# Last layer of a four-part transformer kernel: constant column addresses for TensorE, the weights' transfers placed sooner in SyncE's queue, their splitting placed later on ScalarE and VectorE

## What is computed

```python
# hidden_states = _layernorm(x): 2048 rows of 512
queries = (hidden_states @ W_q).reshape(2, n, 64)
routing = jnp.einsum('tnd,tdk->tnk', queries, keys)          # 2 x n x 64
scores2, idx2 = jax.lax.top_k(routing, 8)
...
scores, pk = jax.lax.top_k(all_scores, 8)                     # the best 8 of 8 x 8 sums
indices = jnp.take_along_axis(all_idx, pk, axis=-1)
de, ue = down_embed[indices], up_embed[indices]               # 8 rows of 512 per token, twice
ew = jnp.einsum('nh,nkh->nk', x, de)
ew = jax.nn.silu(ew) * jax.nn.softmax(scores, axis=-1)
experts_states = jnp.einsum('nk,nkh->nh', ew, ue)
mlp = jax.nn.silu(x @ gate_w) * (x @ up_w) @ down_w           # 512 -> 2048 -> 512
return mlp + experts_states
```

## Time and profile before

| | us |
|---|---|
| median of three runs (2124.6 to 2127.25) | 2127.24 |
| profiled execution, its own time | 2129.43 |
| its span, first to last instruction | 2127.6 |
| TensorE busy in the span | 2019.8 (95%) |
| VectorE busy | 1281.5 (60%) |
| ScalarE busy | 795.7 (37%) |
| GpSimd busy | 518.3 (24%) |
| mean granted TensorE clock | 0.976 of full speed |

### The profile page before, as it was taken

One profiled execution on the slowest core, in us unless ns is written; L12 is line 12 of the kernel. 1 busy time (PEld: TensorE's weight loads), 2 busy tenths in 40 slices (PEclk: granted clock), 3 DMA queues, 4 the chain that ended last, 5 costly groups with the idle time before them and its releaser, 6 DMA issues. The chain is left out here.

```text
span 2127.6 us, 33610 instructions
## 1 busy us (share of the span) xinstructions
PE 2019.8 (95%) x12656; PEld 1658.0 (78%) x12656; DVE 1281.5 (60%) x2270; ACT 795.7 (37%) x2370; POOL 518.3 (24%) x545
## 2 busy tenths in 40 slices
PE   6999999999999989999999999997399999999998
PEld 5888888888888878788877777775277788887887
DVE  5555555755555554424354777764657677775787
ACT  5555555755555532111123545453123222121211
POOL 3222222321233226101022323322200122222321
PEclk9999999999999999999999999999599999999999
DMA  7000000200021013201041000000320455544545
GB/s 253 19 7 5 5 7 15 75 30 28 30 70 58 23 60 89 70 10 59 10 141 50 19 15 22 22 16 21 115 80 2 152 188 188 185 151 154 185 156 191
DMA packets 78565, 158.31 MB, mean 74 GB/s; under 512 B 8848, under 2 KB 31120, under 8 KB 78480
## 3 DMA queue, kind: packets, MB, share of 16 engines
q0 software_dynamic: 23712, 87.04, 12.3%
q1 hardware_dynamic: 54768, 70.17, 10.1%
HBM read 140.41 MB, written 16.78 MB: 74 GB/s over the span
## 5 line engine op out<-in xcount | busy, mean ns | idle before, releaser
L48 PE MATMUL four_banks<-xT_all,m_w_hi 128*128 (+1 forms) x1024 | 321.7, 395 | 1.1 <-PEq L1905 1.1
L2251 POOL DMA_INDIRECT ring<-in_table,x_row x128 | 124.6, 973 | 441.9 <-DVE y_all L2354 312.0
L48 PEld LDWEIGHTS four_banks<-xT_all,m_w_hi 128*128 128x128 f32 x1024 | 193.0, 189 | 46.8 <-issue 1.2
L48 PE MATMUL four_banks<-xT_all,m_w_lo 128*128 (+1 forms) x512 | 202.4, 395 | 0.0
L511 ACT ACTIVATE prob<-four_banks,mx,rms 128x128 f32<-128x128 f32 x256 | 113.9, 462 | 92.4 <-DVE mx L645 92.4
L1120 DVE TENSOR_SCALAR f_relu<-bank,f_b 128x512 f32<-128x512 f32 x64 | 48.0, 749 | 163.5 <-ACT f_h_hi L1063 163.5
L1063 ACT ACTIVATE f_h_hi<-bank,f_b 128x512 fp32r<-128x512 f32 x64 | 44.1, 689 | 258.8 <-PE bank L48 258.8
L289 POOL TENSOR_TENSOR rms<-ssq,constants 128x8 f32<-128x8 f32 x64 | 13.0, 204 | 434.5 <-ACT junk L496 262.2
L48 PE MATMUL bank<-m_w_hi,m_prod_hi 128*128 128x512 f32 x256 | 103.4, 404 | 14.8 <-DVE m_prod_lo L2277 14.8
L1787 DVE TENSOR_REDUCE l_roped<-four_banks 128x16 f32<-128x2048 f32 x32 | 73.4, 2294 | 70.4 <-PE four_banks L1474 70.1
L48 PEld LDWEIGHTS four_banks<-xT_all,m_w_lo 128*128 128x128 f32 x512 | 96.2, 188 | 23.1
(11 more groups left out here) (290 smaller groups left out, 5361.4 us busy)
## 6 DMA issues: line engine op xcount, KB each, us to landing
f_stage<-in_w POOLq DMA_DIRECT2D x14, 512.0 KB, 4.5
f_x_in<-x SPq DMA_DIRECT2D x18, 256.0 KB, 3.0
ctx_in<-in_ctxT SPq DMA_DIRECT2D x32, 128.0 KB, 2.6
x_in<-in_x SPq DMA_DIRECT2D x16, 256.0 KB, 2.6
x<-xres SPq DMA_DIRECT2D x16, 256.0 KB, 2.0
x<-l_res SPq DMA_DIRECT2D x16, 256.0 KB, 2.1
m_stage<-in_gate SPq DMA_DIRECT2D x8, 512.0 KB, 5.1
m_stage<-in_up SPq DMA_DIRECT2D x8, 512.0 KB, 7.0
```

Source lines behind the costliest of these rows:

```text
L48: mm = pe.matmul(out, st, mv, start=first and n == 0, stop=last and n == len(terms) - 1)
L2251: pool.indirect_dma_start(ring[:, slot, :], None, table, bass.IndirectOffsetOnAxis(ap=row[:, tile_of(g), k:k + 1], axis=0)).then_inc(S[f"g ...
```

## The change

The column of `xT_all` becomes a constant slice. TensorE's chunk loops are written out: a double pair (8 steps) is one body, once written out and once inside the loop over three double pairs. On SyncE the transfers of pair p move from position 8(p-1)+4 to 8(p-1)-1, ahead of `load_x` at the same position. On ScalarE `cut(p)` moves from half-step 8(p-1)+2 to 8(p-1)+3, behind that half-step's silus. On VectorE the three thirds move from half-steps 8(p-1)+3, +4, +5 to +4, +5, +6, and within the half-step from ahead of the routing or experts to behind them.

```diff
@@ sync
-                if n // (2 * NC) + 1 == pair and n % (2 * NC) == NC and pair < PAIRS:
+                if n == 2 * NC * (pair - 2) + 7 and pair < PAIRS:
                     load_weights(pair)
@@ tensor
-                col = pe.snap(c * CH)
-                return [[xT_all[part][:, k, bass.ds(col, CH)] for part in range(2)] for k in range(KD)]
+                cols = slice(c * CH, (c + 1) * CH)
+                return [[xT_all[part][:, k, cols] for part in range(2)] for k in range(KD)]
...
-            with pe.Fori(1, NC) as c:
-                step(c, c, 0, 0)
-            pe.wait_ge(S["w_cut"], CUTS)
-            step(NC, 0, 1, 0)
-            with pe.Fori(1, NC) as c:
-                step(NC + c, c, 1, 1)
+            def two_pairs(o):
+                for slot in range(2):
+                    for c in range(NC):
+                        n = (2 * o + slot) * NC + c
+                        if c == 0 and not (isinstance(o, int) and o == 0 and slot == 0):
+                            pe.wait_ge(S["w_cut"], (2 * o + slot) * CUTS)
...
+                            step(n, c, slot, slot if c else 1 - slot)
+            two_pairs(0)
             with pe.Fori(1, PAIRS // 2) as o:
-                for slot in range(2):
-                    pair = 2 * o + slot
-                    pe.wait_ge(S["w_cut"], pair * CUTS)
-                    step(pair * NC, 0, slot, 1 - slot)
-                    with pe.Fori(1, NC) as c:
-                        step(pair * NC + c, c, slot, slot)
+                two_pairs(o)
@@ scalar
-                    if j == 0 and n % NC == 1 and n // NC + 1 < PAIRS:
+                    if j == 1 and n % NC == 1 and n // NC + 1 < PAIRS:
                         cut(n // NC + 1)
@@ vector
-            CUT_AT = ((1, 1), (2, 0), (2, 1))
+            CUT_AT = ((2, 0), (2, 1), (3, 0))
...
                         add_y(n - 1)
                         dve.wait_ge(S["y_added"], TPC * n)
-                    if (n % NC, j) in CUT_AT and n // NC + 1 < PAIRS:
-                        cut_lo(n // NC + 1, CUT_AT.index((n % NC, j)))
                     if n < ROUTES:
                         (choose, find_rows)[j](n)
                     for g in taken[2 * n + j]:
...
+                    if (n % NC, j) in CUT_AT and n // NC + 1 < PAIRS:
+                        cut_lo(n // NC + 1, CUT_AT.index((n % NC, j)))
```

More of the change, by code:

```diff
@@ L2185, in step @@
                 down(n, slot, 0)
-            gate_and_up(0, 0, 0, 0, first=True)
-            gate_and_up(0, 0, 0, 1, first=True)
-            down(0, 0, 0, first=True)
-            with pe.Fori(1, NC) as c:
-                step(c, c, 0, 0)
-            pe.wait_ge(S["w_cut"], CUTS)
-            step(NC, 0, 1, 0)
-            with pe.Fori(1, NC) as c:
-                step(NC + c, c, 1, 1)
-            with pe.Fori(1, PAIRS // 2) as o:
-                for slot in range(2):
-                    pair = 2 * o + slot
-                    pe.wait_ge(S["w_cut"], pair * CUTS)
-                    step(pair * NC, 0, slot, 1 - slot)
-                    with pe.Fori(1, NC) as c:
-                        step(pair * NC + c, c, slot, slot)
+            def two_pairs(o):
[4 more added lines that the diff above has]
+                            pe.wait_ge(S["w_cut"], (2 * o + slot) * CUTS)
+                        if isinstance(n, int) and n == 0:
+                            gate_and_up(0, 0, 0, 0, first=True)
+                            gate_and_up(0, 0, 0, 1, first=True)
+                            down(0, 0, 0, first=True)
+                        else:
+                            step(n, c, slot, slot if c else 1 - slot)
+            two_pairs(0)
+            with pe.Fori(1, PAIRS // 2) as o:
+                two_pairs(o)
             down(STEPS - 1, 1, J - 1)
```

## The result

| | before | changed |
|---|---|---|
| median of 8 runs, us | 2127.40 | 2117.74 |
| lowest and highest | 2124.60, 2132.05 | 2112.81, 2119.78 |
| profiled execution | 2129.43 | 2117.98 |
| its span | 2127.6 | 2116.2 |
| layer's start in the span | 1564.09 | 1565.28 |

The ratio on record is 0.9946, 95% interval 0.9934 to 0.9959: 0.5% faster, by 8.7 to 14.0 us, with 11.5 in the middle. It is worked out from all runs and not from the two medians, which lie 9.7 us apart. The forecast was 2114.5 in a range of 2108 to 2121, a gain of 12.7 us. In the two profiled executions, one of each kernel, the layer's matmuls got 556.78 - 544.15 = 12.6 us shorter. The layer also began 1.2 us later, in code that the change does not touch, so the span shrank by 11.4.

What follows compares the result with a forecast made beforehand. TensorE was taken as the bound, so only its waits and lost clock could be won. The terms -14.7 - 0.2 + 2.2 = -12.7 us took the profiled 2129.43 to 2116.7, hence a median of 2114.5 us, range 2108 to 2121.

Steps and rivals of the forecast that it cites:

- The bound and the two long waits: TensorE bounds; its waits at h = 11 and 43, with lost clock, go once SyncE issues transfers sooner: -14.7 us.
- The high part later: ScalarE's cut one half-step later: silu(3) starts at 1597.31 and the first of five waits, at down(3), goes.
- The low parts behind the routing: VectorE's thirds in pair 1: down(5) waits 1.3 us, gates(8) 5.1 us; routing steps change by -0.2 us.
- the lost clock: TensorE's lower clock level behind the wait at gates(8): 2.3 us, the mean of 2.62 and 2.05.
- The low parts behind the experts: VectorE's last third comes late at pairs 3, 4 and 5: new waits 1.28 + 0.22 + 0.70 = +2.2 us.
- Constant columns, loops: TensorE's constant columns and written-out loops: 0 us; bounds for the two backward branches 0 and 2 x 7.4 us.
- The sum: All terms over the whole kernel: -14.7 - 0.2 + 2.2 = -12.7 us.
- the step from the profiled execution to the median: Whole kernel: profiled execution taken to stand 2.2 us above the median, so 2116.7 becomes 2114.5 us.
- the one case that was priced: TensorE's 5.1 us wait at gates(8), taken to cost clock like the two long waits, 2.3 us.

Runs made afterwards that it cites:

- x1: Kernel before with only SyncE's line changed, transfers of pair p at position 8(p-1)-1; layer 541.97 us, ratio 0.9936.
- x7: Kernel before with the transfers of pair p at position 8(p-1)+2 of SyncE's program, not +4; layer 541.96 us, ratio 0.9931.
- x4: Changed kernel with ScalarE's cut back in half-step 8(p-1)+2; layer 546.67 us, ratio 0.9961.
- x3: Changed kernel with the thirds of the low parts ahead of the routing or experts, in the same half-steps; layer 539.31 us, ratio 0.9930.
- x6: Changed kernel with pair 1's last third at the end of half-step 5, not 6; layer 542.75 us, ratio 0.9936.
- x5: x3 with pair 1's cut ahead of ScalarE's exp in half-step 2 and its thirds behind choose(1) and choose(2) on VectorE; layer 535.93 us, ratio 0.9907.
- x2: Kernel before with only TensorE's program changed, constant columns and chunk loops written out; layer 554.1 us, ratio 1.0000.

## Why the prediction was right

**The bound and the two long waits.** Right, with cause and size: 14.7 us forecast, 14.8 measured by x1. x7 shows the cause that was read off the chain, `load_x` at the head of SyncE's queue.

**The high part later.** Right: down(3) no longer waits, and x4 gives the part's own worth, 2.5 us. I had not priced it by itself; in the sum it is inside the chain from silu(3) to gates(8).

**The low parts behind the routing.** Right step by step. Down(5) was forecast to wait 1.3 us, it waited 1.03 of recorded idle (1.2 by start to start). The last third was forecast to be seen 70.2 us behind the layer's start and was seen at 1635.38 - 1565.28 = 70.1. The wait was forecast at 5.1, recorded at 4.67 of idle (4.8 by start to start); the lost clock at 2.3, measured at 1.8 (7.40 for 5.59). Down(7) at 78.1 was forecast, 77.3 measured, for 78.3 before, so the routing steps gained 0.9 us and not 0.2. The step that was mis-sized is the lost clock.

**The low parts behind the experts.** The places were right: pairs 3, 4 and 5, none at 2, 6 and 7. Forecast 1.28, 0.22 and 0.70; by start to start 1.39, 0.89 and 0.60. They sum to 2.9 in place of 2.2, and the missing 0.7 is the gather that a dot product of half-step 29 waited for. From down(7) to the layer's end the changed kernel takes 466.8 us and x1 and x3, without these waits, 463.7: by that measure they cost 3.1. x3 removes these waits together with the one at gates(8).

**Constant columns, loops.** 0 forecast, 1.0000 measured. The range of this cost had an upper end of 14.8 us that no run came near. The prediction took the earlier trace rows for two returns of the old body; they cover one, and the trace from 1830 us on covers both. For TensorE, the Trainium skill's two-page rule (Runtime: NRT & Kernel Launch, Instruction fetch mechanics) has the traces against it, also for the doubled body: no 16 KB fetch after 1830 us. The Trainium skill's 128 KB for TensorE (Advanced Engine Details and Errata, ISA Cache) fits both bodies; no run here had one larger.

**The sum.** Layer: 12.7 forecast, 12.6 measured. Part of this closeness is luck. The terms were forecast at -14.7, -0.2 and +2.2 and came out at -14.8, -0.9 and +3.1, so two errors of 0.7 and 0.9 us cancel.

The median came out 3.2 us above the forecast all the same. The profiled execution was forecast at 2116.7 and took 2117.98, which is 1.3 more: the 1.2 us by which the layer began later, and 0.1. The other 2.0 are the step from the profiled execution to the median. It was taken as 2.2 us from the kernel before, where it only tells how far that one execution lay above its median; for the changed kernel it is 0.2. Over the profiled executions of all nine kernels, whose code ahead of the layer is the same, the layer's start lies between 1561.6 and 1566.7 us. That spread is wider than every term of the sum but the two waits. What varies there stays open. The ratio, 11.5 us, is the fairer measure, since it uses all runs of both kernels.

**What was mis-sized in the reasoning.** The prediction priced the clock by the length of the wait: lost from 1.86 us on. That is wrong; the last section has the rows. It did no harm to the sum, since the one case that was priced did lose it.

## What to carry to other kernels

Before counting an engine as late, look at what stands at the head of the queue that feeds it: here two small loads, each waiting for the work of the very half-step that wanted the weights, each held 1.5 MB of them. In layer time one line was worth more than the whole change. When work is moved later on an in-order engine, follow that engine's chain to the semaphore's count, not only to the half-step in which it stands; a third of 1.2 us behind `choose(3)` made TensorE wait 4.7 us and lose clock. When it was moved, the next wait took over most of that, and 1.4 us were won (x6). Put such work where the engine already waits for another one, as x5 does beside exp and its table load.

## What was not expected of the hardware

The length of a wait does not tell whether TensorE's clock falls to its lower level (1.2 of 2.4 GHz). In the kernel before it fell behind waits of 2.24 and 1.86 us, which the windows view shows as a granted clock of 0.90 in each of these two stretches:

```profile
1597.40:1614.10 16.70, 14.46 (x56) 11.29 (x55) 11.73 (x29) 6.17 (x7) 0.00 (x0) 0.90 0.00 0
1614.10:1630.70 16.60, 14.74 (x57) 11.56 (x56) 12.45 (x55) 5.14 (x7) 0.00 (x0) 0.90 0.00 0
```

In x2 it stayed at 1.00 through waits of 2.14 and 1.60 us late in the layer, in x3 through 2.18 and 3.43, and in x6 it fell around one of 3.03. The granted clock has to be read in each run. Where it fell behind one of these waits, the cost was 1.5 to 1.7 us; behind the 4.67 us at gates(8) it was 1.8.

The second surprise is how exact such sums are while one engine's chain is followed with durations from the same trace: for x1, x3, x5 and x7 they came within 0.4 us of 540. For x3 that was the sum alone; its split into waits and clock was wrong.
